# Second layer norm applied on VectorE, first-layer weight pieces split in other slots of the attention loop

## The reference

```
x = x + tanh(g_xattn) * xattn(layernorm(x), ctx)      # 16 heads of 8
n = layernorm(x)
x = x + tanh(g_ffn) * (shared_ffn(n) + routed_ffn(n) + n)
```

## Time and profile before

| | us |
|---|---|
| median of 3 runs (431.93 to 433.79) | 432.69 |
| the profiled execution | 434.03 |
| its span, first to last instruction | 432.2 |

### The profile page before, as it was taken

How to read it: one execution, slowest core, us unless ns; L and a number is a source line. 1 busy time by engine, 2 the same in 40 slices (tenths; PEclk the granted TensorE clock), 3 DMA queues, 4 the chain that set the end, 5 groups by cost and what they waited for, 6 DMA issues and landing times.

```text
span 432.2 us, 11933 instructions
## 1 busy us (share of the span) xinstructions
PE 377.4 (87%) x3840; PEld 334.1 (77%) x3840; DVE 296.3 (69%) x968; ACT 273.7 (63%) x609; POOL 265.2 (61%) x263
## 2 busy tenths in 40 slices
PE   3378999899999899999899986699999999999950
PEld 2256868787878788878899985598999998999850
DVE  4555766787778768776669875477776663577863
ACT  4248798888889877888666543465565666554500
POOL 8910312267878757765978976106666666777771
PEclk9769999999999989999999999999999999999985
DMA  4449874537465435455677687677888893133322
GB/s 140 128 120 209 263 203 126 158 114 213 130 184 159 147 114 175 148 154 178 187 230 215 194 264 247 198 218 219 257 242 238 258 256 113 52 101 92 87 79 68
DMA packets 67974, 74.33 MB, mean 172 GB/s; under 512 B 10469, under 2 KB 59237, under 8 KB 67913
## 3 DMA queue, kind: packets, MB, share of 16 engines
q1 hardware_dynamic: 59304, 56.84, 45.6%
q0 software_dynamic: 6800, 14.46, 11.8%
q10 hardware_dynamic: 1808, 2.28, 1.6%
HBM read 43.69 MB, written 29.29 MB: 169 GB/s over the span
## 4 chain that ended last, share of the span: by engine, by line
PE 42%; POOL 16%; DMA 13%; issue 9%; DVE 6%; ACT 6%; SPq 5%; ACTq 2%; DVEq 1%; POOLq 0%
POOL k_heads L620 8%; PE psum L1453 8%; PE psum L1324 8%; PE psum L1341 6%; PE psum L1304 3%; PE psum L1443 3%; DMA xn<-in_packs 3%; DMA ctx_buf<-in_packs 2%; POOL q_stack L620 2%; PE psum L1444 2%; PE psum L1445 2%; DMA k_parts<-in_packs 2%; DMA q_stack<-q_split 2%; ACT probs L705 2%; PE psum L1433 2%
## 5 line engine op out<-in xcount | busy, mean ns | idle before, releaser
L553 POOL DMA_INDIRECT rows_by_expert<-xn_all,row_of x96 | 94.9, 989 | 38.8 <-issue 17.6
L705 ACT ACTIVATE probs<-psum 77x512 f32<-77x512 f32 x128 | 68.9, 589 | 6.1 <-PE psum L1324 4.7
L620 POOL DMA_INDIRECT k_heads<-outs_by_block,back_row x60 | 57.4, 957 | 24.8 <-issue 15.2
L893 DVE TENSOR_REDUCE max_cols<-psum 128x4 fp32r<-128x312 f32 x128 | 55.3, 473 | 9.4 <-PE psum L1304 9.4
L1443 PE MATMUL psum<-q_parts,w_ring 128*128 128x256 f32 x152 | 48.7, 321 | 11.0 <-ACT probs L797 9.1
L1324 PE MATMUL psum<-q_stack,k_heads 128*77 128x128 f32 x512 | 55.5, 245 | 1.5 <-ACT q_stack L697 1.4
L1324 PEld LDWEIGHTS psum<-q_stack,k_heads 128*77 128x77 f32 x512 | 44.2, 151 | 14.6 <-issue 6.3
L1031 DVE CAST w_ring<-w 128x512 fp32r x76 | 35.9, 472 | 24.4 <-issue 18.4
L789 ACT ACTIVATE q_parts<-psum 128x256 fp32r<-128x256 f32 x76 | 29.1, 385 | 24.7 <-PE psum L1433 19.1
L1304 PE MATMUL psum<-k_heads,q_stack 128*128 128x312 f32 x128 | 35.6, 358 | 10.5 <-DMA q_stack<-q_parts 7.1
L1019 DVE TENSOR_TENSOR q_parts<-psum,q_parts 128x256 fp32r<-128x256 f32 x76 | 31.9, 421 | 18.4 <-ACT q_parts L789 16.2
(11 more groups left out here) (160 smaller groups left out, 916.7 us busy)
## 6 DMA issues: line engine op xcount, KB each, us to landing
w_raw<-rows_by_expert SPq DMA_DIRECT2D x76, 128.0 KB
outs_by_block<-probs SPq DMA_DIRECT2D x76, 128.0 KB
q_stack<-q_split SPq DMA_DIRECT2D x21, 256.0 KB
k_heads<-k_split SPq DMA_DIRECT2D x90, 39.0 KB
rows_by_expert<-zeros SPq DMA_DIRECT2D x24, 128.0 KB, 4.9
q_split<-q_parts SPq DMA_DIRECT2D x6, 512.0 KB
k_split<-k_parts SPq DMA_DIRECT2D x8, 312.0 KB, 2.3
xn<-in_packs SPq DMA_DIRECT2D x19, 129.0 KB
```

Of the source, the lines that this page charges most:

```text
L553: nc.gpsimd.indirect_dma_start(xd[:, :], bass.IndirectOffsetOnAxis(ap=row_of[:, r, m:m + 1], axis=0), xn2_all[:, r * GB + m // K, :], None ...
L620: nc.gpsimd.indirect_dma_start(back[j][:, k * GB + b, :], None, yd[half][:, :], bass.IndirectOffsetOnAxis(ap=back_row[:, j, b * K + k:b * ...
L705: nc.scalar.activation(probs[0:KV, n % 2, hg * 512:(hg + 1) * 512], st_ps[hg % 2][0:KV, :], ACT.Exp, scale=SCALE).then_inc(exp_done, 1)
L893: nc.vector.tensor_reduce(max_cols[:, n % 2, hg * HQ:(hg + 1) * HQ], s_ps[hg % 2][:, 0:HQ * KP].rearrange("q (h k) -> q h k", h=HQ), AX.X, ...
```

## The change

Three edits. `shift2` and its semaphore go; VectorE applies the second norm itself, as subtract the mean and multiply by `rstd2`, behind `stats2_of` in the slots o = 2 and o = 3 (for the last group at u = 4 and 5, with `shift2_of` gone from u = 3). The w1 pieces are split in slots 1, 2, 3 and 23 to 28. `stats1_of` runs at o = 0 and `var1_of` at o = 1 (for g = 0 both stay at o = 2).

```diff
+    W1_AT = (1, 2, 3, 23, 24, 25, 26, 27, 28)
...
 # GpSimd's loop
-                if t % 3 == 0 and 1 <= t // 3 <= PIECES:
-                    trail_w1(t // 3 - 1)
+                if t in W1_AT:
+                    trail_w1(W1_AT.index(t))
...
 # ScalarE's loop: apply2 goes from o == 2 and o == 3 and from u = 4, 5
-                if t % 3 == 0 and 1 <= t // 3 <= PIECES:
-                    lead_w1(t // 3 - 1)
+                if t in W1_AT:
+                    lead_w1(W1_AT.index(t))
...
 # VectorE
-            def shift2_of(r):
+            def apply2(r, first, end):
                 dve.wait_ge(ln2_rstd, r + 1)
-                if r >= 1:
-                    dve.wait_ge(xn2_ready, r * GB)
-                nc.vector.scalar_tensor_tensor(shift2[:], mv2[:, :, 0:1].rearrange("p b a -> p (b a)"), -1.0, rstd2[:], ALU.mult, ALU.mult).then_inc(shift2_ready, 1)
+                for b in range(first, end):
+                    ins = nc.vector.tensor_scalar(xn2_all[:, r * GB + b, :], tile(r * GB + b), mv2[:, b, 0:1], rstd2[:, b:b + 1], ALU.subtract, ALU.mult)
+                ins.then_inc(xn2_ready, end - first)
...
-                if o == 2 and 1 <= g < NG:
-                    shift2_of(g - 1)
...
                 if t >= 2:
                     stats2_of(t - 2)
+                if o == 2 and g >= 1:
+                    apply2(g - 1, 0, 2)
+                if o == 3 and g >= 1:
+                    apply2(g - 1, 2, GB)
                 if o == 3 and g >= 2:
                     weigh(g - 2)
                 if o == 2 and g >= 2:
                     place(g - 2)
-                if o == 2 and g + 3 < NG:
+                if g + 3 < NG and (o == 2 if g == 0 else o == 0):
                     stats1_of(g + 3)
+                if g + 3 < NG and (o == 2 if g == 0 else o == 1):
                     var1_of(g + 3)
...
 # VectorE's expert loop
-                if u == 3:
-                    shift2_of(NG - 1)
+                if 4 <= u < 6:
+                    apply2(NG - 1, (u - 4) * 2, (u - 3) * 2)
```

More of the change, by code:

```diff
@@ L105, in flamingo_kernel @@
         mv1, mv2 = (sb(n, [P, GB, 2]) for n in ("mv1", "mv2"))
-        var1, rstd1, shift1, var2, rstd2, shift2 = (sb(n, [P, GB]) for n in ("var1", "rstd1", "shift1", "var2", "rstd2", "shift2"))
+        var1, rstd1, shift1, var2, rstd2 = (sb(n, [P, GB]) for n in ("var1", "rstd1", "shift1", "var2", "rstd2"))
         zero_rows = sb("zero_rows", [P, P], F32R)
@@ L259, in flamingo_kernel @@
         ln2_rstd = sem("ln2_rstd")
-        shift2_ready = sem("shift2_ready")
         xn2_ready = sem("xn2_ready")
@@ L678, in apply1 @@
                 ins.then_inc(xn_ready, end - first)
[L680 to L684, removed]
             def x2T_leaves(r):
@@ L760, in _ @@
                     apply1(g + 2, 0, 2)
-                if o == 3 and 1 <= g < NG:
-                    apply2(g - 1, 2, GB)
                 if t == 0:
@@ L777, in _ @@
                     lead_k(g + 2)
-                if o == 2 and 1 <= g < NG:
-                    apply2(g - 1, 0, 2)
                 if o == 3 and g >= 1:
                     x2T_leaves(g - 1)
-                if t % 3 == 0 and 1 <= t // 3 <= PIECES:
-                    lead_w1(t // 3 - 1)
+                if t in W1_AT:
+                    lead_w1(W1_AT.index(t))
             def lead_rows(u):
@@ L813, in _ @@
                     onT_leaves(B - 1)
-                if 4 <= u < 6:
-                    apply2(NG - 1, (u - 4) * 2, (u - 3) * 2)
                 if u == 7:
```

## The result

The changed kernel takes 454.69 us (451.72 to 457.36, four runs), the kernel before beside it 433.24; the ratio is 1.0487 [1.0436, 1.0539]. It is slower by 21 us, where +14.15 was forecast, and its median lies 1.2 us above the top of the forecast's range, 453.5. The four times fall into two pairs, near 452 and near 457 us; the lower pair would have been inside the range. The profiled execution is one of the upper pair: it took 457.31 us, its span is 455.4.

The account below looks back on a forecast made before the run. The prediction took TensorE's own work to bound the kernel, so gaps there count; 7.75 + 8.4 + 1.6 + 0.7 - 2.0 - 0.7 - 1.6 = +14.15 us on 434.03 gave 448.2 profiled, 446.8 median, range 440 to 453.5.

Parts of the forecast that it names:

- Piece 0 in slot 1: Slots 1 to 3: ScalarE waits for piece 0's load, TensorE's clock falls, 1.4 comes back in slot 3; +7.75 us.
- `apply2` at o = 3: Slots 7, 11, ... 31: `turn_x2` waits for the second half of `apply2` on VectorE, +1.2 us seven times; +8.4.
- `stats1_of`: Slots 8, 12 and 16, o = 0: statistics ahead of `add_bias` delay `values` by 0.5 us each; +1.6.
- GpSimd in slots 23 to 28: Six pieces instead of two put GpSimd behind; `pow2` of slot 26 comes 1 to 3 us later, delaying `place`; +0.7.
- rival D: Last group, u = 4: a GpSimd power holds up `apply2` to its end, up to 5 us added; 451.8; chance 0.03.
- Gains: TensorE's waits shrink: for `maxima` net of `place` -2.0 us, for ScalarE's maxima rows -0.7, at the expert blocks -1.6.
- B, the clock: Gaps at o = 3 or GpSimd's standstill lower TensorE's clock, 1.05 us each; 450 to 456, middle 452; chance 0.16.
- C, faster: VectorE's release from GpSimd at o = 2 decides if the load and `turn_x2`'s input are ready; 425.9 us; chance 0.04.

Follow-up runs that it names:

- early_only: The kernel before with only the first three w1 pieces moved to slots 1, 2 and 3; 437.97 us, ratio 1.0085.
- early2: The kernel before with the first three w1 pieces in slots 2, 4 and 5 instead of 3, 6 and 9; 433.91 us, ratio 1.0022.
- stats_only: The kernel before with only the first norm's statistics moved, `stats1_of` to o = 0 and `var1_of` to o = 1; 434.12 us, ratio 1.002.
- late_only: The kernel before with only the last six w1 pieces in slots 23 to 28; 437.2 us, ratio 1.0083.
- after_no25: The changed kernel with the piece of slot 25 in slot 22; 450.03 us, ratio 1.0391.
- after_turn_early: The changed kernel with the second norm's second pair of tiles ahead of the residual addition on VectorE; 440.86 us, ratio 1.0231.
- apply_early: The kernel before with only the second norm applied on VectorE, its second pair of tiles ahead of the residual addition; 429.43 us, ratio 0.9936.
- late_gap: The kernel before with the last six w1 pieces in slots 21, 22, 23, 26, 27, 28; 436.5 us, ratio 1.0116.
- w_off_o1: The kernel before with the pieces of slots 9 and 21 moved to 8 and 20; 431.95 us, ratio 0.9976.
- pool_extra: The kernel before, no piece moved, with two unused 128x4 powers added on GpSimd in each of slots 23, 25, 26 and 28; 440.42 us, ratio 1.0201.

## Why the prediction was wrong

By its own steps, with what the trace of after and the single parts show:

1. *Piece 0 in slot 1* (+7.75): the mechanism is right. ScalarE waited 5.98 us in after and 6.86 in early_only; slots 2 and 3 together are 7.1 us longer in after. In early2, one slot later, the wait came out within 0.14 us of the same reckoning. The agreement of the sum is in part luck: the 1.4 that was to come back in slot 3 is not steady (4.62 us in stats_only, where nothing there was moved, 5.87 before). By time the three early pieces cost 5.1, as they free slot 10; the step left that out.
2. *`apply2` at o = 3* (+8.4): right in its place, a little small in its size. The seven waits are 1.4 to 1.5 us (9.8 in all, +1.2 forecast each), since the pair starts as said but takes 0.6, not 0.48. Not seen was how cheaply it could be cured.
3. *`stats1_of`* (+1.6, where three times the forecast's own 0.5 is 1.5): 1.1 by the waits, 1.3 by slots 9, 13 and 17 of stats_only (0.43 each).
4. *GpSimd in slots 23 to 28* (+0.7, at most 2.8): **this step failed.** Slots 26 to 28 are 7.8 us longer, of which 1.4 is part 2: 6.4 us. The step had the backlog (1 to 3 us at the root of slot 26; 3.1 measured in after, 3.3 in late_only) and looked only at `place` behind it. It missed that a piece's subtraction holds up VectorE, though the forecast names such a lock for the last group (rival D), and that TensorE's clock would be at half speed for 14 us behind it.
5. *Gains* (-2.0, -0.7, -1.6): the waits for the maxima went (slots 6, 10, 22 and 30 are 0.93, 0.84, 1.56 and 0.70 us shorter, 4.0 in all). In slots 10 and 22 the moved pieces alone give as much (0.92 in early_only, 1.38 in late_only), so it is not the norm's merit only. `place` is later by 0.36 in four slots and by 0.62 in slot 31, 2.1 in all (0.1 each in four was forecast): -1.9 net, against -2.0, with both halves larger than forecast. The step from block 5 to block 6 went from 3.42 to 1.81 us (-1.6). The -0.7 for ScalarE can't be told apart from slot 3.

With the measured values, 7.1 + 9.8 + 1.1 - 1.9 - 1.6 = 14.5 us, as large as the forecast's sum. The trace has 23.2 more than before. The other 8.7 are slots 26 to 28 (6.4), slot 8 (1.3) and slot 31 beyond its two waits (1.4), both with the clock low, less 0.4 that is spread over the rest.

Of the rivals, *B, the clock*, came nearest: 450 to 456. In windows of 1 us, after runs at 1.2 GHz in five stretches between the start-up and the last 15 us, near 44, 75, 187, 218 and 276 us, and before in one, near 152. The falls near 75 and 218 us come as the second pair's gaps of 1.38 us end, as B says, but the other five of those seven gaps start none (four at the full clock, one with the clock already low), and the price B gave part 4 was 2 us. The long one is bound to parts 2 and 4: it is gone without the piece in slot 25 (after_no25) and 3 us instead of 14 long without the pair's wait in slot 27 (after_turn_early). *C, faster*, was given 0.04, and its condition, that `turn_x2` finds its input, was the right one: apply_early meets it and takes 429.43. *D, a lock* at the last group, did not happen. The pair ran in 0.59 us inside GpSimd's power (timeline, expert blocks):

```profile
233.98 6.56 POOL L625 TENSOR_TENSOR expd<-euler,shifted 128x36 f32<-128x36 f32 x1
```

```profile
234.77 0.59 DVE L913 TENSOR_SCALAR xn_all<-x_all,mv,rstd 128x128 f32<-128x128 f32 x2
```

Left open: why after's four times fall into two pairs, and why late_gap's time is above its trace. For the first, one fall of the clock more or less would do it: the mean granted clock was 0.935 and 0.929 in the runs of 457 us and 0.941 and 0.949 in those of 452. But only the run of 457.31 has a trace.

## What to carry to other kernels

When work moves to an engine whose queue runs in order, ask first which consumer it serves and what stands ahead of it there: the same pair of 0.6 us, seven times in the kernel, cost 13 us more behind an instruction that waits for that consumer's engine than ahead of it. An engine at 60% busy is no place to put work without looking at the next step on it that others wait for; here a root behind the scatters. And a list of slots for background work wants checking against both: which step it delays, and which short instruction of VectorE runs beside it.

## What the runs showed of the hardware

The subtraction on GpSimd (128x512, both inputs in SBUF, 1.28 us) holds up some instructions of VectorE to its end: a tensor_scalar of 128x39 took 1.52 and 1.75 us (0.30), a pair of 128x128 1.58 (0.6), a tensor_tensor of 128x72 with both inputs in SBUF 2.00 (0.21). The reductions from PSUM keep their 0.86. The trace of before has all of this beside the instruction of the earlier trace rows: a subtraction that starts 0.05 us behind it and takes 1.38, a reduction that keeps its length, and a small instruction with two SBUF inputs, 0.21 us in the earlier trace rows, that takes 0.46 and ends with the subtraction (timeline, before):

```profile
48.50 1.38 POOL L559 TENSOR_TENSOR w<-w_raw,w 128x512 fp32r<-128x512 f32 x1 [1.79 <-ACT w L722]
48.65 0.87 DVE L893 TENSOR_REDUCE max_cols<-psum 128x4 fp32r<-128x312 f32 x2
49.43 0.46 DVE L872 SCALAR_TENSOR_TENSOR shift<-mv,rstd 128x4 f32<-128x4 f32 x1
```

The Trainium skill, page "SBUF — State Buffer", section "Who interferes with whom", says that a VectorE instruction with two SBUF inputs contends with a GpSimd instruction that reads SBUF, that `tensor_scalar` can enter a two-port mode, which contends with GpSimd too, and that `tensor_reduce` never does on this chip. These lengths agree. The section also says that whoever issues first gets the ports; that these rows don't settle, for in slot 26 of after the held instruction starts 0.18 us ahead of the subtraction (183.69 and 183.87), in late_only 0.42 and in w_off_o1 0.60, each time with a scatter of GpSimd running until the subtraction starts. The forecast set the rule aside after one row with a power. The power still shows no lock in after, at 233.98; for the subtraction the rule holds, and reading it for the six late pieces would have put lengths of 1.3 us beside part 4.

A short stall costs more than itself when TensorE's clock falls behind it: in after the granted clock was 0.50 from 187.7 to 201.6 us, and slots 27 and 28 took 9.35 and 6.98 us where after_no25 has 5.99 and 5.11. But the length of a gap told neither whether the clock falls nor for how long. The gaps of 0.92 and 0.46 us ahead of slot 23's `values` were followed by a fall in before and in pool_extra, and by none in stats_only, early_only, early2 and late_gap. In pool_extra a gap of 1.78 us in slot 26 brought none. The gap of 6.2 us in slot 2 of after was followed by some 7 us at the lower clock. The one of 0.94 in slot 26, with 0.66 and 1.39 us of idle time to come in the low stretch itself, was followed by 14. In after_turn_early gaps of 1.19 and 0.65 in slot 26, with none for the pair in slot 27, were followed by 3. So a forecast can price a fall from rows, but these traces give no rule for when one comes.
